# A clear and a wait for it ahead of each gather of a graph layer's main loop

## What is computed

```python
xn = _layernorm(x, axis=-1)
# graph part: 32 relations, 8 bases
weight = einsum('rb,bio->rio', w_comp, bases)
msg = einsum('ni,rio->nro', xn, weight)[src, edge_type] * edge_weight
gnn = relu(segment_sum(msg, dst, num_segments=6250))
x = x + gnn + mix(xn[None])[0]            # mix: linear attention, 8 heads, and its two-layer network
x = x + ffn(_layernorm(x)[None])[0]       # ffn: 8 experts, three matrices each, weighted by a softmax
```

## Time and profile before

| | |
|---|---|
| median of the runs | 4206.27 us |
| the profiled execution, its own time | 4209.15 us |
| its span, first to last instruction | 4207.4 us |
| TensorE matmul busy | 3357.9 us, 80% |
| VectorE busy | 2255.9 us, 54% |
| GpSimd busy | 1949.4 us, 46% |
| ScalarE busy | 800.3 us, 19% |
| mean granted TensorE clock | 0.92 |
| moved by DMA | 864 MB, 205 GB/s |

### The profile page before, as it was taken

The page is one execution under the profiler, slowest core; times in us unless marked ns, Lnnn a source line. Parts: engine busy times, 40 slices in busy tenths (PEclk is TensorE's granted clock), DMA queues, the critical chain, the costliest instruction groups (busy, mean ns, idle before and its releaser), DMA issues.

```text
span 4207.4 us, 68614 instructions
## 1 busy us (share of the span) xinstructions
PE 3357.9 (80%) x18778; PEld 2955.5 (70%) x18778; DVE 2255.9 (54%) x6008; ACT 800.3 (19%) x1546; POOL 1949.4 (46%) x2001
## 2 busy tenths in 40 slices
PE   0179976686988889898898888888888888888887
PEld 0157765575877868788787787877877778777675
DVE  5634465555555565555555555555555555555422
ACT  0023420001112121121211212112121221211233
POOL 0132246655555555555555555555454555555100
PEclk9999987887999999999899998998989999899899
DMA  6467776666766667676676766767667676676532
GB/s 195 128 194 237 241 206 189 198 194 207 235 206 219 211 219 239 201 230 208 210 232 208 229 210 209 228 217 226 204 210 231 214 219 216 208 237 207 163 103 80
DMA packets 647245, 864.29 MB, mean 205 GB/s; under 512 B 63829, under 2 KB 524195, under 8 KB 646686
## 3 DMA queue, kind: packets, MB, share of 16 engines
q1 hardware_dynamic: 510962, 549.74, 40.0%
q0 software_dynamic: 95776, 262.27, 21.8%
q10 hardware_dynamic: 40140, 47.81, 3.4%
HBM read 551.97 MB, written 316.84 MB: 206 GB/s over the span
## 4 chain that ended last, share of the span: by engine, by line
PE 53%; issue 11%; DVE 9%; another core or an unknown queue 5%; ACT 3%; DVEq 1%; SPq 0%; DMA 0%; ACTq 0%
PE PS L1674 53%; DVE steps L1306 4%; ACT feed L926 1%; DVE steps L1270 1%; DVE feed L1602 1%; ACT h_high L925 0%; ACT mixbuf L902 0%; DVE h_low L1005 0%; PE PS L1743 0%; ACT mixbuf L896 0%; DVE lst L1415 0%; DVE mixbuf L1437 0%; DVE lnr L1005 0%; DVE mixbuf L1005 0%
## 5 line engine op out<-in xcount | busy, mean ns | idle before, releaser
L746 POOL DMA_INDIRECT steps<-normed_nodes,steps x1968 | 1931.2, 981 | 1781.9 <-PE PS L1674 877.3
L1306 DVE SCALAR_TENSOR_TENSOR steps<-steps,PS 128x256 f32<-128x256 f32 x1968 | 944.7, 480 | 1599.5 <-PE PS L1674 1107.1
L1674 PE MATMUL PS<-steps 128*128 128x128 f32 x7872 | 1267.4, 299 | 316.6 <-issue 133.3
L1674 PEld LDWEIGHTS PS<-steps 128*128 128x128 f32 x7872 | 1169.1, 211 | 422.6 <-issue 257.7
L926 ACT ACTIVATE feed<-PS,bnc 128x512 f32<-128x512 f32 x416 | 319.9, 774 | 825.5 <-PE PS L1674 547.4
L1674 PE MATMUL PS<-bases_s,feed 128*128 128x256 f32 x1664 | 440.7, 408 | 0.0
L1674 PEld LDWEIGHTS PS<-bases_s,feed 128*128 128x128 f32 x1664 | 416.4, 334 | 6.2
L1270 DVE TENSOR_TENSOR steps<-steps 128x512 f32<-128x512 f32 x494 | 337.3, 683 | 0.1
L1674 PE MATMUL PS<-w_one,feed 128*128 128x256 f32 (+1 forms) x1028 | 309.5, 427 | 5.8 <-ACT feed L926 5.8
L925 ACT ACTIVATE h_high<-PS,bnc 128x512 fp32r<-128x512 f32 x208 | 161.6, 777 | 794.5 <-PE PS L1674 724.4
L1674 PE MATMUL PS<-h_high,split_in 128*128 128x512 f32 x832 | 276.0, 458 | 16.8 <-ACT feed L926 16.7
(11 more groups left out here) (208 smaller groups left out, 2881.3 us busy)
## 6 DMA issues: line engine op xcount, KB each, us to landing
step_sums<-steps SPq DMA_DIRECT2D x492, 512.0 KB
split_in<-expert_split SPq DMA_DIRECT2D x104, 1024.0 KB
feed<-step_sums SPq DMA_DIRECT2D x416, 128.0 KB
steps<-step_types SPq DMA_DIRECT2D x125, 256.0 KB
steps<-normed_nodes,steps POOLq DMA_INDIRECT x1968
mixbuf<-mix_hidden SPq DMA_DIRECT2D x53, 256.0 KB
w_zero<-in_L_ffn_Wo_dram SPq DMA_DIRECT2D x52, 256.0 KB
w_one<-in_L_ffn_Wo_dram SPq DMA_DIRECT2D x52, 256.0 KB
```

The source lines that it names most:

```text
L746: pool.indirect_dma_start(out=ring[:, k, :], out_offset=None, in_=xnD, in_offset=bass.IndirectOffsetOnAxis(ap=idxc[:, u, k:k + 1], axis=0) ...
L1306: dve.scalar_tensor_tensor(acc[:, k % ACCR, :], acc[:, (k - 1) % ACCR, :], keepc[:, k:k + 1], PS[:, slot(k):slot(k) + C], ALU.mult, ALU.ad ...
L1674: return pe.matmul(o, a, b, start=start, stop=stop)
```

## The change

A tile `hold` of 8 words on each of the 128 partitions is added. In `steps`, after the wait for the ring's slot and ahead of each gather, GpSimd clears this tile, with a signal on a new semaphore `held`, and then waits for this signal, again with the helper that makes the wait an instruction of its own. Nobody reads the tile or the semaphore otherwise.

```diff
         flag = sb("flag", [1, 1], I32)
+        hold = sb("hold", [P, 8])
         flagf = sb("flagf", [P, 1])
...
                 for k in range(UN):
                     wait_apart(pool, "mm_done", it * UN + k + 1)
+                    pool.memset(hold[:, :], 0.0).then_inc(sem("held"), 1)
+                    wait_apart(pool, "held", it * UN + k + 1)
                     pool.indirect_dma_start(out=ring[:, k, :], out_offset=None, in_=xnD,
```

## The result

The changed kernel takes 4437.97 us, the median of four runs (4432.65 to 4443.68), beside 4208.26 us for the kernel before on the same chip (four runs). The ratio is 1.055, 95% interval 1.053 to 1.058: 230 us slower, where some 370 were forecast. The profiled execution took 4443.68 us, its span is 4441.9 us.

What follows compares the result with a forecast made beforehand. GpSimd was to become the bound after 599 us: 1840 gathers at 2.02 us each put the last gather at 4316 us; 263 us of tail and 1.8 us around the span gave 4580 us, range 4440 to 4820.

Steps and rivals of the forecast that it cites:

- The bound: Main loop: GpSimd's turn of 2.02 us exceeds the wanted 1.61 and 1.84 us after 600 us, not the first stage's 2.92.
- The sequencer's 0.77 us: On GpSimd, from granted wait to gather start: hidden beside the gather before, 0.77 us exposed per gather by the change.
- The rival of the hidden sequencer: On GpSimd, the 0.77 us stays mostly hidden: turn 1.55 us, time 4209 us; chance 0.10.
- gather: First term of GpSimd's turn: the gather itself, 0.98 us, the mean from the trace.
- from its end to the clear: Second term of GpSimd's turn: gather end to clear start, taken as 0.10 us, between 0.07 and 0.30.
- clear: Third term of GpSimd's turn: the clear of 8 words, taken as 0.12 us.
- signal and way to the next gather: Fourth and fifth terms of GpSimd's turn: signal to the sequencer 0.05 us, granted wait to gather start 0.77 us.
- The tail: After the last gather to the span's end: 283 us before, some 20 of it going, so 263 us.
- the range for the turn: GpSimd's time per gather when slots are free: 1.95 to 2.10 us, chance 0.70 for the forecast.
- The clock: Rival on TensorE: more idle time lowers its granted clock to 0.79, making it slower than GpSimd, 4723 us; chance 0.08.
- 1.61 and 1.84 us a gather: Main loop's demand from 600 to 1000 us and from 1000 us on, read from the profile's windows.

Runs made afterwards that it cites:

- e7: Changed kernel with clear and wait only in the first 24 of 123 iterations; 4338.48 us beside 4273.89 for the kernel before, ratio 1.014.
- e8: Changed kernel with clear and wait only in the first 6 iterations; 4262.88 us beside 4273.89 for the kernel before, ratio 0.997.
- e1: Changed kernel with clears kept (2 words each) but no wait ahead of each gather, only once in 16; 3743.02 us beside 3740.47 before, ratio 1.0006.
- e2: Changed kernel, but each wait is for the clear one gather back; 3740.67 us beside 3740.47 for the kernel before, ratio 1.0001.
- e3: Changed kernel without the clear: the sequencer raises the signal itself, then waits for it; 3740.79 us beside 3740.47 for the kernel before, ratio 1.000.
- e9: Changed kernel with the wait for the ring's slot put behind the clear's wait; 4617.26 us beside 4273.89 for the kernel before, ratio 1.079.
- e10: The changed kernel as it is, on another chip; 4441.37 us beside 4273.53 for the kernel before, ratio 1.039.
- e4: Changed kernel with clear and wait ahead of odd steps only; 3931.34 us beside 3740.47 for the kernel before, ratio 1.052.
- e11: Changed kernel with clear and wait ahead of odd steps only, on another chip; 3950.53 us beside 4273.53 for the kernel before, ratio 0.925.
- e12: Changed kernel with clear and wait ahead of every fourth step only; 4190.14 us beside 4273.53 for the kernel before, ratio 0.981.
- e5: Changed kernel with clear and wait done twice ahead of each gather; 5030.52 us beside 4273.89 for the kernel before, ratio 1.176.

## Why the prediction was right, and where it was off

*The bound.* GpSimd became the bound behind 600 us and not before: right, by the chain, by TensorE's waits for rows, and by e7 and e8.

*The mechanism.* The sequencer's 0.77 us come into the open because the wait can't be met before the running gather has ended: right. The distance from grant to gather is the 0.77 us of the earlier trace rows again; e1 clears the clear, e2 and e3 the wait as such, e9 shows it from the other side. The rival of the hidden sequencer fell. "DMA: Bandwidth & Descriptors" of the Trainium skill, section "Anatomy of one DMA — SWDGE (gpsimd) path", has about 50 ns for this dispatch. The trace doesn't agree: from the granted wait to the gather it is 0.77 us here, 0.56 of them to the sequencer's own next instruction.

*The sizes.* Step by step, predicted and measured in the stages behind 600 us: gather 0.98 and 0.994; from its end to the clear 0.10 and 0.00; clear 0.12 and 0.121; signal and way to the next gather 0.05 + 0.77 = 0.82 and 0.833 on average (0.809 in most turns). Sum 2.02 and 1.949. So the mis-sized term is the second. I had bounded it by 0.07 from below and taken 0.10, from the rows of a small direct DMA and of iotas; here it is 0.00, outside of the bounds. "Perfetto Trace Analysis" of the Trainium skill, section "GPSIMD Engine Instruction", advises to time GpSimd's instructions by the distance of their starts rather than by recorded spans. The trace bears that out in one point: behind a gather's recorded end a clear starts after 0.00 us and another gather after 0.30, so the gap that I took from a small direct DMA didn't carry over. Over 1840 gathers 0.071 us are 131 us: 4316 - 131 = 4185, the measured start of the last gather. The tail was 256 us where I had 263. Together these are 138 us; the forecast span of 4579 is 137 over 4441.9. The lower end of the range for the turn, 1.95 us, was the true value, in part by luck: the second term lay 0.07 us below its lower bound, and the others lay as much above theirs (gather 0.01, clear 0.02, signal and way 0.03). The forecast of 4580 was 142 us too high, and 4438 lies just below the 4440 that I gave as the range's lower end.

*The clock.* TensorE's granted clock in the middle stage fell from 0.79 to 0.71, and over the long stage from 0.93 to 0.91:

```profile
600.00:1000.00 400.00, 263.59 (x1291) 239.27 (x1291) 182.56 (x499) 18.00 (x46) 227.45 (x415) 0.71 0.56 169
1000.00:4185.00 3185.00, 2596.34 (x14313) 2312.41 (x14313) 1707.01 (x4437) 564.10 (x963) 1823.76 (x3266) 0.91 0.65 204
```

(Both rows are of the changed kernel.) These are means between the levels of 1.2 and 2.4 GHz. TensorE was 66% busy in the middle stage before and after, 86% and then 82% in the long one, and nothing shows that the clock cost time: with a turn of 1.95 us TensorE waits for rows, as that rival said of a partial loss.

*What I read wrongly.* I took 1.61 and 1.84 us a gather as what the loop wants, a property of TensorE's work. On chips without late signals it is 1.33 and 1.62. The rows for it stood in the profile of before, 326 us of "remote" and 205 us of "issue", and I passed them over because the chain has them as 5% and 11% without a line. It didn't hurt this forecast, as the turn of 1.95 us is over either value, and the changed kernel has no late signals. But it means that the 230 us are a balance: of the 495 us of late signals before, 3 are left after, and the slower gathers cost that much more. That the late signals would go was no part of the forecast. Against 3740 us the changed kernel would be 19% slower; it wasn't run on such a chip, and this is worked out from the same 4440 us on two others.

## What to carry to other kernels

GpSimd's wait for its own work wasn't priced by the round trip of the signal, 0.03 us here, but by the way from the granted wait to the gather, which had lain beside the running gather: 0.77 us for each, and 0.10 us for a further wait put behind it. Waiting for the clear one gather back cost nothing. On another engine none of this was measured. Before a pace read from a trace is used as demand, look whether "issue" and "remote" make up part of it, and on which chip it was read: the same edit, at every second gather, gave -7.5% on one chip and +5.2% on another.

## What the runs showed that I hadn't expected

- The kernel before takes 3740, 4208 or 4274 us by the chip (or the job), while the kernels paced by GpSimd agree to 0.1% (4438 and 4441, e10) or 0.5% (3931 and 3951, e4 and e11).
- On two of the three kinds of chip TensorE's signals come some 2.5 us late on average, about 200 times in an execution, 495 to 530 us in sum, for the kernel before or nearly so. In e7 they are absent while gathers are held to one in 1.88 us and return after; e12, with one gather in four held, keeps them all. What in TensorE, or on the way of its signals, holds them back isn't shown, nor whether the gathers' rate or the sequencer's running ahead brings them on. TensorE's granted clock goes with the time, 0.92 in the profile of before and 0.95 in that of e3; the kernel of every second gather has 0.93 and 0.95 (e11 and e4) where its times are nearly equal, so a lower clock of the chip itself doesn't show.
- Where before takes 4274 us, a clear with a wait at every second gather (e11) is the fastest kernel of all that ran, 3951 us. Where it takes 3740, none was faster than before, and e1 to e3 took the same.
- A loop body of GpSimd that was 144 instructions longer than the changed kernel's (48 times a clear, its wait and the arithmetic for it, e5) stood 1.84 us at the end of nearly each trip.
